# Mask of the turned scores in two PSUM banks, one bank for the turned scores, and a new order of the attention's engine lines

## The reference

```python
# x, ctx: (8, 128, 512); H, KVH, D = 32, 8, 128; each k/v head serves 4 q heads
q = rope(layernorm(x) @ Wq); k = rope(ctx @ Wk); v = ctx @ Wv
scores = q @ k^T / sqrt(128)
scores = where(mask == 0, -1e9, scores)
o = softmax(scores) @ v @ Wo
x = x + tanh(g_xattn) * o
x12 = layernorm(x) @ w12^T + b12;  x1, x2 = split(x12, 2)
out = x + tanh(g_ffn) * ((silu(x1) * x2) @ w3^T + b3)
```

## Time and profile before

| what | value |
|---|---|
| time, 3 runs | 745.94 us median (741.55 to 746.91) |
| the profiled execution | 743.0 us, of which the profile's span is 741.2 |
| mean granted TensorE clock in the span | 0.949 of full speed |
| DMA | 118.38 MB, mean 160 GB/s |
| MATMUL instructions in the span | 2865 |

### The profile page before, as it was taken

The page is one execution under the profiler, slowest core; times in us unless marked ns, Lnnn a source line. Parts: engine busy times, 40 slices in busy tenths (PEclk is TensorE's granted clock), DMA queues, the critical chain, the costliest instruction groups (busy, mean ns, idle before and its releaser), DMA issues.

```text
span 741.2 us, 10094 instructions
## 1 busy us (share of the span) xinstructions
PE 654.7 (88%) x2865; PEld 530.2 (72%) x2865; DVE 583.8 (79%) x1235; ACT 318.3 (43%) x892; POOL 453.8 (61%) x374
## 2 busy tenths in 40 slices
PE   8999999969677888688878787887888999999998
PEld 7888888748566667566666575676666788888886
DVE  3887657897889879788889788887798788989352
ACT  4347324643433444434434444343434455764320
POOL 6359669877665766566667766765765767741010
PEclk9999999999898999898999899998999999999999
DMA  9988952635554655364546465555445442400002
GB/s 310 317 261 279 335 173 102 191 126 176 166 192 148 203 180 173 111 220 146 162 151 207 134 190 180 172 175 180 153 159 155 153 119 74 99 0 1 1 15 99
DMA packets 133990, 118.38 MB, mean 160 GB/s; under 512 B 9776, under 2 KB 104496, under 8 KB 133936
## 3 DMA queue, kind: packets, MB, share of 16 engines
q1 hardware_dynamic: 132512, 116.69, 49.8%
q0 software_dynamic: 384, 1.05, 0.4%
q10 hardware_dynamic: 1040, 0.00, 0.1%
HBM read 72.89 MB, written 44.83 MB: 159 GB/s over the span
## 4 chain that ended last, share of the span: by engine, by line
PE 62%; issue 12%; DVE 12%; POOL 9%; ACT 2%; DMA 2%; POOLq 0%; DVEq 0%; ACTq 0%
PE o_bank L889 8%; PE o_bank L890 7%; PE o_bank L891 7%; PE f_bank L889 7%; PE f_bank L890 7%; PE f_bank L891 7%; DVE prob L2511 7%; PE pv_bank L889 3%; PE pv_bank L891 2%; POOL q L2001 2%; PE pv_bank L890 2%; POOL q_lo L1961 2%; PE s_banks L889 2%; PE s_banks L891 2%; PE s_banks L890 2%
## 5 line engine op out<-in xcount | busy, mean ns | idle before, releaser
L1491 ACT ACTIVATE prob<-prob,small 128x128 f32<-128x128 f32 x256 | 99.7, 391 | 185.4 <-DVE small L2511 175.1
L2010 POOL TENSOR_TENSOR prob<-prob,small 128x512 f32<-128x512 f32 x64 | 66.7, 1043 | 135.7 <-DVE small L2542 130.6
L889 PE MATMUL o_bank<-wo_hi,o_hi 128*128 128x512 f32 x248 | 108.3, 437 | 45.4 <-issue 44.9
L2511 DVE CUSTOM_DVE_ANT_0 prob<-s,mfill 128x128 f32<-128x128 f32 x192 | 144.3, 803 | 1.6 <-DMA s<-s_scratch 1.5
L890 PE MATMUL o_bank<-wo_lo,o_hi 128*128 128x512 f32 x248 | 105.0, 423 | 0.0
L891 PE MATMUL o_bank<-wo_hi,o_lo 128*128 128x512 f32 x248 | 104.5, 421 | 0.0
L889 PE MATMUL f_bank<-xT_hi,wq_hi 128*128 128x512 f32 x256 | 100.8, 394 | 0.1
L891 PE MATMUL f_bank<-xT_hi,wq_lo 128*128 128x512 f32 x256 | 100.1, 391 | 0.0
L890 PE MATMUL f_bank<-xT_lo,wq_hi 128*128 128x512 f32 x256 | 100.1, 391 | 0.0
L889 PEld LDWEIGHTS o_bank<-wo_hi,o_hi 128*128 128x128 f32 x248 | 52.0, 210 | 64.1 <-issue 53.2
L2001 POOL TENSOR_TENSOR q<-t_cos,t_sin 128x512 f32<-128x512 f32 x64 | 83.5, 1307 | 15.7 <-DVE t_sin L2414 15.5
(11 more groups left out here) (183 smaller groups left out, 1459.4 us busy)
## 6 DMA issues: line engine op xcount, KB each, us to landing
p_scratch<-p_blk SPq DMA_DIRECT2D x51, 256.0 KB, 2.0
p<-p_scratch SPq DMA_DIRECT2D x51, 256.0 KB, 3.3
s_scratch<-s_blk SPq DMA_DIRECT2D x48, 256.0 KB, 2.1
s<-s_scratch SPq DMA_DIRECT2D x48, 256.0 KB, 3.2
k_scratch<-ks_parts SPq DMA_DIRECT2D x16, 512.0 KB, 3.1
raw<-in_L_xattn_Wq_dram SPq DMA_DIRECT2D x32, 256.0 KB, 3.6
raw<-in_L_xattn_Wo_dram SPq DMA_DIRECT2D x32, 256.0 KB, 3.6
k_parts<-k_scratch SPq DMA_DIRECT2D x16, 512.0 KB, 4.9
```

Of the source, the lines that this page charges most:

```text
L889: nc.tensor.matmul(dst, st[0], mv_[0], start=start, stop=False)
L1491: e = nc.scalar.activation(prob[:, k, h, :], prob[:, k, h, :], ACT.Exp, bias=nmin[k][:, h:h + 1], scale=-1.0, accum_out=psum_row[k][:, h:h ...
L2010: nc.gpsimd.tensor_tensor(prob[:, k], prob[:, k], rrow[k].unsqueeze(2).to_broadcast([128, GH, S]), ALU.mult).then_inc(pool_norm, 1)
L2511: op = nc.vector.tensor_tensor_reduce(prob[:, k, h, :].rearrange("p (j a) -> p j a", j=4), scores[:, h], fill, 1.0, HUGE, ALU.add, ALU.min ...
```

## The change

The edit of the code:

```diff
-        mfill2 = place("mfill2", [128, B, S], F32, at["cT_lo"] + 8192)
+        mask_bank = [t_bank[:, :], s_banks[:, 512:1024]]
 # PE, scores
                 if turned(n):
-                    if n < ST0 + 2:
+                    if n == ST0:
                         pe.wait_ge(dve_mask, ST0)
                     else:
-                        pe.wait_ge(dve_sblk, n - 1 - ST0)
-                    three(s_banks[:, 512 * k:512 * k + 512], ...
+                        pe.wait_ge(dve_sblk, n - ST0)
+                    three(s_banks[:, 0:512], ...
...
                 if n == ST1:
                     pe.wait_ge(dve_sblk, ST1 - ST0)
+                    pe.wait_ge(dve_mask, ST1 - HB)
 # ACT
-            def mask_columns():
-                act.wait_ge(pe_v, 16)
-                act.wait_ge(pe_kq, ROT_ORDER.index(("K", KVH - 1, 1)) + 1)
-                act.wait_ge(dve_small, 4)
-                nc.scalar.activation(mfill2[:, :, :].rearrange("p b (j a) -> p b a j", j=4), mfill[:, :, :].rearrange("p b (a j) -> p b a j", j=4),
-                                     ACT.Copy).then_inc(act_mask2, 1)
+            def mask_columns(half):
+                if half:
+                    act.wait_ge(dve_mask, ST0)
+                else:
+                    act.wait_ge(dve_pTlo, HEAD_T)
+                hi(mask_bank[half].rearrange("p (b j a) -> p b a j", b=HB, j=4),
+                   mfill[:, HB * half:HB * half + HB, :].rearrange("p b (a j) -> p b a j", j=4), act_mask2)
 # DVE, score_blocks
-                                    s_banks[:, 512 * k:512 * k + 512].rearrange("p (h i b) -> p i h b", h=GH, i=4)).then_inc(dve_sblk, 1)
+                                    s_banks[:, 0:512].rearrange("p (h i b) -> p i h b", h=GH, i=4)).then_inc(dve_sblk, 1)
 # DVE, mask_turned
+                elif n == ST0 + HB:
+                    dve.wait_ge(act_mask2, 2)
...
-                fill = mfill2[:, n % B, :].rearrange("p (j a) -> p j a", j=4)
+                fill = mask_bank[n % B // HB].rearrange("p (b j a) -> p b j a", b=HB, j=4)[:, n % HB]
                 for h in range(GH):
-                    op = nc.vector.tensor_tensor_reduce(prob[:, k, h, :].rearrange("p (j a) -> p j a", j=4), scores[:, h], fill, 1.0, HUGE,
+                    op = nc.vector.tensor_tensor_reduce(prob[:, k, h, :].rearrange("p (j a) -> p j a", j=4), fill, scores[:, h], 1.0, HUGE,
                                                         ALU.add, ALU.min, nmin[k][:, h:h + 1])
```

The order of the calls is new in all five queues from n = 1 to the end; each call is still made once, and no DMA is added or left out. In the middle of the attention PE now runs, for instance:

```diff
             scores(*u(20))
             q_block(0, 25)
-            out_proj(*u(16))
             pv(*u(17))
+            out_proj(*u(16))
             scores(*u(21))
             q_block(0, 26)
-            q_block(0, 27)
-            pv(*u(18))
+            out_proj(*u(17))
             scores(*u(22))
-            out_proj(*u(17))
+            pv(*u(18))
+            q_block(0, 27)
             out_proj(*u(18))
-            pv(*u(19))
             scores(*u(23))
```

More of the change, by code:

```diff
@@ L1132, in _ @@
             prob_transpose(0, 0, 1)
+            q_block(0, 8)
             scores(0, 1, 1)
-            q_block(0, 8)
             q_block(0, 9)
+            pv(0, 0, 1)
+            scores(0, 2, 0)
             out_proj(0, 0, 0)
-            scores(0, 2, 0)
-            pv(0, 0, 1)
             scores(*u(5))
             q_block(0, 10)
-            out_proj(*u(1))
+            q_block(0, 11)
             pv(*u(2))
             scores(*u(6))
-            q_block(0, 11)
+            out_proj(*u(1))
+            scores(*u(7))
+            out_proj(*u(2))
+            pv(*u(3))
             q_block(0, 12)
-            scores(*u(7))
-            pv(*u(3))
-            out_proj(*u(2))
             out_proj(*u(3))
@@ L1164, in _ @@
             q_block(0, 16)
+            scores(*u(12))
             out_proj(*u(7))
-            scores(*u(12))
             pv(*u(8))
+            q_block(0, 17)
+            out_proj(*u(8))
+            pv(*u(9))
             scores(*u(13))
-            q_block(0, 17)
             q_block(0, 18)
+            out_proj(*u(9))
             scores(*u(14))
-            pv(*u(9))
-            out_proj(*u(8))
             pv(*u(10))
-            out_proj(*u(9))
             q_block(0, 19)
+            pv(*u(11))
             out_proj(*u(10))
-            pv(*u(11))
             scores(*u(15))
@@ L1216, in _ @@
             q_block(0, 29)
-            scores(*u(25))
             pv(*u(21))
             out_proj(*u(20))
+            scores(*u(25))
             q_block(0, 30)
+            out_proj(*u(21))
             pv(*u(22))
@@ L1284, in _ @@
             q_block(0, 46)
-            q_block(0, 47)
-            pv(*u(38))
             scores(*u(42))
             out_proj(*u(37))
+            pv(*u(38))
+            q_block(0, 47)
+            out_proj(*u(38))
             pv(*u(39))
-            out_proj(*u(38))
             scores(*u(43))
@@ L2343, in _ @@
             norm(3, 6, 1)
+            norm(3, 7, 0)
             ffn_lo(4)
-            norm(3, 7, 0)
             ffn_lo(5)
@@ L2702, in _ @@
             sin_q(17)
+            add_out(*u(8))
             p_blocks(*u(11))
@@ L2705, in _ @@
             mask_turned(*u(12))
+            o_lo_split(*u(9))
+            recip(*u(12))
             cos_q(0, 18)
-            o_lo_split(*u(9))
             sin_q(18)
+            p_blocks(*u(12))
+            add_out(*u(9))
             score_blocks(*u(14))
-            recip(*u(12))
-            add_out(*u(8))
-            p_blocks(*u(12))
             mask_turned(*u(13))
@@ L2727, in _ @@
             p_blocks(*u(14))
+            add_out(*u(11))
             score_blocks(*u(16))
@@ L2767, in _ @@
             p_blocks(*u(19))
+            add_out(*u(16))
             score_blocks(*u(21))
@@ L2778, in _ @@
             o_lo_split(*u(18))
-            add_out(*u(17))
+            recip(*u(21))
             cos_q(0, 27)
-            recip(*u(21))
             sin_q(27)
@@ L2784, in _ @@
             score_blocks(*u(23))
+            add_out(*u(18))
             mask_turned(*u(22))
@@ L2802, in _ @@
             o_lo_split(*u(21))
+            add_out(*u(20))
+            recip(*u(24))
             cos_q(0, 30)
             sin_q(30)
[L2805 removed]
+            p_blocks(*u(24))
+            add_out(*u(21))
             score_blocks(*u(26))
[L2807 to L2808 removed]
+            mask_turned(*u(25))
             o_lo_split(*u(22))
[L2810 to L2811 removed]
+            cos_q(0, 31)
             recip(*u(25))
[L2813 removed]
             sin_q(31)
+            p_blocks(*u(25))
+            add_out(*u(22))
             score_blocks(*u(27))
[L2816 removed]
             mask_turned(*u(26))
             o_lo_split(*u(23))
[L2819 removed]
             recip(*u(26))
@@ L2823, in _ @@
             p_blocks(*u(26))
+            add_out(*u(23))
             score_blocks(*u(28))
@@ L2826, in _ @@
             o_lo_split(*u(24))
-            add_out(*u(23))
             cos_q(0, 33)
@@ L2839, in _ @@
             p_blocks(*u(28))
+            add_out(*u(25))
             score_blocks(*u(30))
@@ L2842, in _ @@
             o_lo_split(*u(26))
-            add_out(*u(25))
             cos_q(0, 35)
@@ L2846, in _ @@
             sin_q(35)
+            add_out(*u(26))
             p_blocks(*u(29))
@@ L2849, in _ @@
             o_lo_split(*u(27))
-            add_out(*u(26))
             mask_turned(*u(30))
@@ L2874, in _ @@
             o_lo_split(*u(30))
-            add_out(*u(29))
+            recip(*u(33))
             cos_q(0, 39)
-            recip(*u(33))
             sin_q(39)
@@ L2903, in _ @@
             p_blocks(*u(36))
+            add_out(*u(32))
+            add_out(*u(33))
+            score_blocks(*u(38))
             o_lo_split(*u(34))
-            score_blocks(*u(38))
             mask_turned(*u(37))
@@ L2930, in _ @@
             o_lo_split(*u(37))
-            add_out(*u(36))
             recip(*u(40))
@@ L2978, in _ @@
             o_lo_split(*u(43))
-            add_out(*u(42))
             recip(*u(46))
@@ L2982, in _ @@
             sin_q(52)
+            add_out(*u(43))
+            p_blocks(*u(46))
             score_blocks(*u(48))
-            p_blocks(*u(46))
+            o_lo_split(*u(44))
             mask_turned(*u(47))
-            o_lo_split(*u(44))
-            add_out(*u(43))
             cos_q(0, 53)
+            recip(*u(47))
             sin_q(53)
-            recip(*u(47))
             p_blocks(*u(47))
+            add_out(*u(44))
             score_blocks(*u(49))
@@ L3014, in _ @@
             sin_q(56)
+            add_out(*u(46))
+            p_blocks(*u(50))
             add_out(*u(47))
-            p_blocks(*u(50))
             mask_turned(*u(51))
```

1044 lines of the change are left out of this document (517 added, 527 removed).

## The result

The kernel after takes 637.31 us (median of 4 runs, 635.01 to 638.01), the kernel before 744.64 in the same rounds. The ratio is 0.8556, with a 95% interval of 0.8514 to 0.8597. I had forecast 647, with 630 to 690 as the range.

A forecast was written before the change was run, and what follows sets the result against it. Masking held behind POOL was taken to leave PE idle or slow in the attention; afterwards PE would be the bound. The sum was 743.0 - 443.5 + 327.1 + 13 + 3 + 4 = 646.6, say 647 us, range 630 to 690.

The forecast's parts named there:

- The cause of the long masking: Line 2511 in the attention: held behind POOL with both inputs in SBUF, not held with one in PSUM.
- PE as the bound: Attention stage after the change: PE sets the pace at 6.80 us a unit, above POOL 6.10 and DVE 5.73.
- The terms of the 20: Attention stage: losses added to PE's 327.1 us, namely 13 for bank and path, 3 for ramp, 4 for gaps.
- One bank and the path together: Turned scores in one bank and the round through DVE: 0.3 us a unit, 13 us over 44 units.
- The ramp: Start of the attention stage, before pv(4): little PE idle left, 3 us.
- The longer gaps with their slow clock: PE in the attention: two or three longer idle gaps, each dropping the clock, 4 us.
- The head and the tail: Stretches before and behind the attention stage, 297.7 us of PE's own work: claimed to stay as they were.
- The price of a PSUM input: Masking instruction on DVE: 36 ns more than uncontended SBUF form, 6.9 us over 192, inside the 0.92 a unit.
- The scores' round trip: Store and load of turned scores through DRAM: 5.3 us, fits into one unit of 6.80 with 1.5 to spare.
- B: Rival: the round through DVE, ACT, POOL and DMA paces the attention, not PE; 683 us (662 to 705), chance 0.19.
- C: Rival: something other than two SBUF inputs, such as access pattern, sets line 2511; 736 to 750 us, chance 0.05.
- D: Rival: one bank for turned scores ties PE to DVE's round, 9.6 us a unit; slower, 760 us, chance 0.04.

The follow-up runs named there:

- e1: Kernel before with the mask in two PSUM banks and one bank for the turned scores, in its old order of calls: 639.94 us, ratio 0.8598.
- e2: Kernel after, new order and one bank for the turned scores, with the mask back in SBUF: 742.67 us, ratio 0.9955.
- e3: Kernel before, old order and two banks, with the mask of sequences 0 to 3 read from PSUM: 698.11 us, ratio 0.9382.
- e9: Kernel before, mask in SBUF, with POOL's long attention instructions cut into two halves each: 722.67 us, ratio 0.9674.
- e4: Kernel after with the masking's two inputs swapped back, scores from SBUF first and mask from PSUM second: 636.00 us.
- e5: Kernel after, one bank for the turned scores, with the mask of sequences 4 to 7 back in SBUF: 691.83 us.
- e6: Kernel after with the mask of sequences 4 to 7 back in SBUF and two banks for the turned scores: 689.75 us.
- e7: Kernel after with the masking done twice in each turned unit, once into a tile nobody reads: 670.26 us, ratio 0.9023.
- e12: Kernel before with the edit of the code, old order, and the masking done twice in each turned unit: 666.51 us, ratio 0.895.
- e8: Kernel after with POOL's remainder of q taken twice in each turned unit, once into a tile nobody reads: 663.88 us.

## Why the prediction was right

**The cause of the long masking.** Right, and shown from four sides: by moving the mask with all else left (e1), by moving it back (e2), by moving half of it (e3), and by shortening what it waits for (e9). Counted over the whole trace of before, 112 of the 192 maskings are held. Each of them starts beside a running POOL instruction and ends 0.14 to 0.15 us behind it. After, 172 start beside a running POOL instruction, and none takes more than 293 ns. That it is not something about the mask's own tiles, two other subtractions of DVE in the kernel before tell, the first with one input in PSUM, the second with both in SBUF:

```profile
L2367 DVE TENSOR_TENSOR o_lo<-pv_bank,o_hi x64: 644/680/693, 137.1 to 665.2; 128x512 fp32r<-128x512 f32 x64
...
L2367 DVE TENSOR_TENSOR wo_lo<-raw,wo_hi x4: 684/833/1362, 39.4 to 51.6; 128x512 fp32r<-128x512 f32 x4
```

The `wo_lo` of 1362 ns starts at 51.59, while POOL's `ks_parts` runs to 52.41. Of the `o_lo`, 24 start beside POOL and take 693 at most.

The Trainium skill, "SBUF — State Buffer", section "Who interferes with whom", says that a VectorE instruction with two SBUF inputs contends with a GpSimd instruction that reads SBUF, and that with at most one, outside the performance modes that use two ports, it does not. The traces agree: up to 1398, 1409 and 1429 ns against 293 at most. That it makes no difference which of the two inputs leaves SBUF is e4's.

**The masking's new size.** Right: 0.92 us a unit forecast, 43.93/48 = 0.92 measured.

**PE as the bound.** Right. PE needs 1437 x 0.2267 = 325.8 us for the instructions that now lie in the stage, and takes 335.1. The loss of 9.3 us stands where I had put 20; 4.1 of it is idle time, and 5.2 are starts a little wider than 0.2267 apart (those right behind an idle come 0.24 to 0.31 apart).

**The terms of the 20.** One bank and the path together, 13 us: too high. PE's idle in the whole stage is 4.1 us, ramp included, and e5 against e6 put the second bank at 2.1 us where DVE is late. The ramp, 3 us, was near: the two longest idles of PE in the stage, 0.92 us at 149.40 and 0.97 at 154.70, come there. The longer gaps with their slow clock, 4 us: there were none, the clock is 1.00. With 9.3 for 20 the sum gives 635.9; the profiled execution took 636.77. The head and the tail, which I had left as they were, came out 2.1 us longer in sum, for the most part by PE work that moved there.

**The price of a PSUM input.** Wrong, though it moved nothing. I took 36 ns for it, from the quickest masking of before (250) against its twin's 286. Both populations have both values: in a series of four the first can take as little as 250, and the other three take 277 to 291 when they are not held, with the mask in PSUM (306.52 and 306.70 above) as in SBUF (308.48 and 308.66 in e9). The median of those other three is 286 with the mask in PSUM and 281 with it in SBUF, so the price is some 5 ns and not 36. The Trainium skill, "VectorE: DVE Perf Modes", section "The TRN2 errata", gives 120 fixed cycles for a PSUM source and 58 for an SBUF source. This case, with one of two inputs moved, does not show that difference.

**DVE's air.** I counted it twice, as 1.07 us by busy time and as 0.4 to 1.1 by the path. e7 says that of 0.92 added 0.69 a unit come through (33/48), so about 0.2 was free: the low end of the path's figure was already too high, and busy time was no guide. In the old order (e12) 27 of the 44 us come through, and about 0.35 was free. POOL's, by busy time, was right (e8).

**The scores' round trip.** Right: it fits into a unit. In the kernel after DVE waited 3.7 us for those loads in the whole run, in 8 places, at 6.98 us a unit.

**The rivals.** B did not happen, but e7 shows how near it is: 0.92 us more of DVE a unit cost 33 us in all. C falls by e2 and e3: the pattern is the same and the place decides. D falls by e1, e5 and e6.

**What stays open.** Whether the new order is worth anything by itself: 0 to 3 us. Why the first of four maskings can be 35 ns quicker than the next was not tried, nor how the 33 us of e7 divide between the waits.

## What to carry to other kernels

Look at the spread of one line's durations: a line of one shape that takes 250 ns at its quickest and 1400 at its slowest may be waiting for something inside the instruction, and the timeline beside it tells for whom. If it is a VectorE instruction with two SBUF inputs beside a busy GpSimd, try one of the two inputs in a PSUM bank, as freed the masking here. A constant such as a mask is cheap to move: two copies by ACT. To tell how much an engine has left, follow the round through its neighbours; its busy share alone promised five times what there was here (1.07 us against 0.2).

## What was not expected

- The old order of the calls, made for units of 9.2 us and two banks, does 639.6 to 639.9 us with the edit of the code alone: no new order was needed to take up the gain.
- A DRAM round trip became the longest wait of the profile, 68.3 us, while PE idles no more than 4.1 us in the stage.
- Cutting POOL's instructions in two took 21 us off the kernel before (744.04 to 722.67) although POOL's own work grew: here a shorter hold was worth more than POOL's time, as POOL was not the bound (352 us busy of the 459 from 140.9 to 600).
